# A two-layer graph network on one core: Pool's gathers wait for the slot superstep that holds the tile five (second loop: seven) tile supersteps back

## The reference, cut to what matters

```python
# layer 0
all_feat = jnp.concatenate([x[dst], x[src], edge_attr, u_per_node[dst]], axis=-1)
msg = jax.nn.relu(all_feat @ W1 + b1)
agg = jax.ops.segment_sum(msg, dst, num_segments=x.shape[0])
x = _layernorm(x + jax.nn.relu(jnp.concatenate([x, agg, u_per_node], axis=-1) @ W2 + b2))
# layer 1
Z = jnp.einsum('ni,rio->nro', h, fc_weight)
z_s = Z[src, etype]; z_d = Z[dst, etype]
e = jax.nn.relu(jnp.sum(jnp.concatenate([z_s, z_d], axis=1) * attn_weight[etype, :, 0], axis=1))
ex = jnp.exp(e - jax.ops.segment_max(e, dst)[dst])
h_out = jax.ops.segment_sum((ex / jax.ops.segment_sum(ex, dst)[dst])[:, None] * z_s, dst)
x = _layernorm(x + h_out)
```

## Time and profile before

| | us |
|---|---|
| median of 3 runs | 5624.8 |
| lowest and highest | 5622.56, 5631.35 |
| the profiled execution, its time | 5585.71 |
| its span, first to last instruction | 5584.0 |

### The profile page before, as it was taken

How to read it: one execution, slowest core, us unless ns; L and a number is a source line. 1 busy time by engine, 2 the same in 40 slices (tenths; PEclk the granted TensorE clock), 3 DMA queues, 4 the chain that set the end, 5 groups by cost and what they waited for, 6 DMA issues and landing times. The chain is left out here.

```text
span 5584.0 us, 71029 instructions
## 1 busy us (share of the span) xinstructions
PE 3080.6 (55%) x17849; PEld 2768.8 (50%) x17849; DVE 2980.1 (53%) x9486; ACT 1278.0 (23%) x4180; POOL 3034.1 (54%) x3265
## 2 busy tenths in 40 slices
PE   2265555455555555545784066555555656655576
PEld 1264444444444444444772055555555555555565
DVE  1265554455555555555773065555555555555567
ACT  0100000000000000000022044444444444444455
POOL 5525555555555555555215706666666666666631
PEclk5555555555555555555566555555555555555555
DMA  3211111111111111111125101111111111111111
GB/s 115 82 45 51 46 53 53 45 51 46 54 52 45 52 46 53 52 44 52 53 100 181 28 27 46 47 47 47 47 47 47 47 47 47 47 47 47 47 38 32
DMA packets 172540, 300.15 MB, mean 54 GB/s; under 512 B 71719, under 2 KB 78235, under 8 KB 158844
## 3 DMA queue, kind: packets, MB, share of 16 engines
q0 software_dynamic: 100032, 105.03, 9.8%
q1 hardware_dynamic: 70662, 188.25, 9.4%
q10 hardware_dynamic: 1462, 2.30, 0.1%
HBM read 260.36 MB, written 34.99 MB: 53 GB/s over the span
## 5 line engine op out<-in xcount | busy, mean ns | idle before, releaser
L453 POOL DMA_INDIRECT ring<-Btab,idx x1563 | 1486.5, 951 | 1214.7 <-DVE XA L846 610.3
L453 POOL DMA_INDIRECT ring<-Ztab,idx x1563 | 1479.9, 947 | 922.2 <-issue 400.0
L719 PE MATMUL p_m<-A,oht 128*128 x1664 | 438.3, 365 | 1061.8 <-DVE full L853 1023.5
L1344 PE MATMUL p_s<-ring,ohx 128*128 x3328 | 808.9, 420 | 191.2 <-issue 187.2
L732 PE MATMUL p_s<-msg,oh 128*128 128x64 f32 x3328 | 763.8, 418 | 178.2 <-issue 137.0
L1344 PEld LDWEIGHTS p_s<-ring,ohx 128*128 128x128 f32 x3328 | 738.8, 325 | 214.4 <-issue 214.1
L732 PEld LDWEIGHTS p_s<-msg,oh 128*128 128x128 f32 x3328 | 731.0, 329 | 204.8 <-issue 204.5
L873 DVE TENSOR_REDUCE p_t<-p_m 128x256 f32<-128x768 f32 x416 | 380.0, 958 | 817.4 <-remote 809.6
L719 PEld LDWEIGHTS p_m<-A,oht 128*128 128x128 bf16 x1664 | 237.6, 145 | 1153.8 <-issue 1109.8
L1402 DVE TENSOR_REDUCE mslot<-p_x 128x8 f32<-128x1024 f32 x208 | 254.7, 1225 | 896.8 <-remote 882.6
L632 ACT ACTIVATE msg<-p_t 128x512 f32<-128x512 f32 x208 | 124.2, 597 | 2552.7 <-issue 2161.9
(11 more groups left out here) (211 smaller groups left out, 2716.4 us busy)
## 6 DMA issues: line engine op xcount, KB each, us to landing
drow<-drow_d SPq DMA_DIRECT2D x104, 1024.0 KB
eaT<-in_eaT_in SPq DMA_DIRECT2D x208, 128.0 KB
Ztab<-Z_stage SPq DMA_DIRECT2D x49, 536.0 KB, 5.1
ring<-Btab,idx POOLq DMA_INDIRECT x1563
ring<-Ztab,idx POOLq DMA_INDIRECT x1563
xTB<-in_xTB_in SPq DMA_DIRECT2D x7, 448.0 KB, 4.0
Btab<-B_stage SPq DMA_DIRECT2D x7, 448.0 KB, 6.0
ring<-in_xTA_in SPq DMA_DIRECT2D x7, 448.0 KB, 4.2
```

What stands on the lines that cost most here:

```text
L453: e.indirect_dma_start(out=ring[:, place(t), :], out_offset=None, in_=table[:, :], in_offset=bass.IndirectOffsetOnAxis(ap=idx[:, t:t + 1], ...
L719: e.matmul(parts(j), OHT[:, s % 2, j, :], A.A3[:, bass.ds(b, 1), :].rearrange("p a c -> p (a c)"), start=True, stop=True)
L1344: last = e.matmul(pS[s % 2][h][:, j % 4, :], OHx[:, s % 2, j, :], ring[:, bass.ds(t, 1), 0:D + 1], start=True, stop=True)
```

## The change

`gathers` gets a third kind of wait, before the first tile of a tile superstep s, from s = `first` on: `used` must have reached a number from a new table, the slot superstep that holds the first slot of tile 8(s - `lead`). In the first loop `lead` is 5 and `first` 10, in the second 7 and 8. The number goes into a register, eight registers are loaded at once for eight tile supersteps, and the wait raises a semaphore `near` that nobody waits for. The old waits stay. In the first loop tile superstep 6 now also waits until `full` is 1.

The table is a new row `A.vrow` of `A.tabs`. For it the count of slots before each tile is kept in `tbef`, turned on PE with the other tables (a sixth transpose at L699 of the new file, on 13 x 128 numbers), cut to each eighth number and shifted right by 3 on DVE into 16 further columns of `rowi`, and loaded by a fourth small DMA on SP. The waits for the tables now want 80 instead of 64.

```diff
-def gathers(e, A, ring, table, idx, s_g, landed, used, summed, free={}):
-
+def gathers(e, A, ring, table, idx, s_g, landed, used, summed, near, name, lead, first, free={}):
+
+    regs = [e.alloc_register(f"{name}{j}") for j in range(O)]
...
         if s >= RT and j == 0:
             e.wait_ge(used, s - RT + BEHIND + 1)
+        if s >= first and j == 0:
+            i = (s - first) % O
+            if i == 0:
+                n = min(O, TO - s)
+                e.reg_load(regs[0:n], A.vrow[0:1, s - lead:s - lead + n])
+            e.wait_ge(used, e.snap(regs[i], min_val=1, max_val=SO)).then_inc(near, 1)
...
-            gathers(e, A, ring, A.Btab, idx, s_g, S["landed"], S["full"], S["acc"], {XT0 // O: (T["a"], len(CHUNKS))})
+            gathers(e, A, ring, A.Btab, idx, s_g, S["landed"], S["full"], S["acc"], S["near"], "l0pg", 5, 10, {6: (S["full"], 1), XT0 // O: (T["a"], len(CHUNKS))})
...
-            gathers(e, A, ring, A.Ztab, idx, s_g, S["landed"], S["s"], S["acc"])
+            gathers(e, A, ring, A.Ztab, idx, s_g, S["landed"], S["s"], S["acc"], S["near"], "l1pg", 7, 8)
...
+            e.dma_start(A.vrow.rearrange("a (c s) -> a c s", c=SC), A.rows_d[:, 3 * P + PER * WX:].unsqueeze(0)).then_inc(T["table"], 16)
...
-                last = e.transpose(pR2[:, r, :], rowsf[:, 4 + r, :], A.ident[:, :])
-            last.then_inc(T["rowt"], 1)
+                e.transpose(pR2[:, r, :], rowsf[:, 4 + r, :], A.ident[:, :])
+            e.transpose(pR2[:, 2, :], tbef[:, :], A.ident[:, :]).then_inc(T["rowt"], 1)
...
-            done(e.tensor_tensor(out=nrel[:, :], in0=w[:, :], in1=pre, op=ALU.add))
-            done(e.tensor_tensor(out=nrel[:, :], in0=nrel[:, :], in1=A.k128[:, :], op=ALU.subtract))
+            done(e.tensor_tensor(out=tbef[:, :], in0=w[:, :], in1=pre, op=ALU.add))
+            done(e.tensor_tensor(out=nrel[:, :], in0=tbef[:, :], in1=A.k128[:, :], op=ALU.subtract))
...
+            done(e.tensor_copy(rowi[:, 3 * P + PER * WX:].unsqueeze(2), by(pR2[:, 2, :])[:, :, 0:1]))
+            e.tensor_scalar(out=rowi[:, 3 * P + PER * WX:], in0=rowi[:, 3 * P + PER * WX:], scalar1=3, scalar2=None, op0=ALU.arith_shift_right)
```

More of the change, by code:

```diff
@@ L493, in phase_layer0 @@
         rowsf = sb("rows_f", [P, 6, SC], F32)
-        rowi = msg[0:SC, :, :, :].rearrange("p a j d -> p (a j d)")[:, 0:3 * P + PER * WX].bitcast(I32)
+        rowi = msg[0:SC, :, :, :].rearrange("p a j d -> p (a j d)")[:, 0:3 * P + PER * WX + PER].bitcast(I32)
         rowx = rowi[:, 3 * P:3 * P + PER * WX].rearrange("p (s w) -> p s w", w=WX)
+        tbef = sb("t_slot", [P, SC], F32)
         bf0, bl0, nt, w, nrel, n2, negm, h2, nb128 = (sb("t_" + n, [P, SC], F32) for n in (
@@ L515, in phase_layer0 @@
         pR = pM[0:SC, 0, :].rearrange("p (r k) -> p r k", r=4)
-        pR2 = pM[0:SC, 1, 0:2 * P].rearrange("p (r k) -> p r k", r=2)
+        pR2 = pM[0:SC, 1, 0:3 * P].rearrange("p (r k) -> p r k", r=3)
         pL = [pM[:, 1 + i, :].bitcast(BF16).rearrange("p (m k) -> p m k", k=P) for i in range(2)]
@@ L519, in phase_layer0 @@
         A3v = A.A3[:, 0:NB, :].rearrange("p (q h) c -> p q h c", h=2)
-        names = "oht oh c m0 m1 full pre msg s acc landed".split()
+        names = "oht oh c m0 m1 full pre msg s acc landed near".split()
         S = {n: sem("l0_" + n) for n in names}
@@ L541, in _ @@
             e.dma_start(wrow[0:1, :, :].rearrange("a (c s) w -> a c (s w)", c=SC), A.rows_d[:, 2 * P:3 * P].unsqueeze(0)).then_inc(T["table"], 16)
-            e.dma_start(xrow[0:1, :, :].rearrange("a (c s) w -> a c (s w)", c=SC), A.rows_d[:, 3 * P:].unsqueeze(0)).then_inc(T["table"], 16)
+            e.dma_start(xrow[0:1, :, :].rearrange("a (c s) w -> a c (s w)", c=SC), A.rows_d[:, 3 * P:3 * P + PER * WX].unsqueeze(0)).then_inc(T["table"], 16)
+            e.dma_start(A.vrow.rearrange("a (c s) -> a c s", c=SC), A.rows_d[:, 3 * P + PER * WX:].unsqueeze(0)).then_inc(T["table"], 16)
             e.wait_ge(T["ix"], 1)
@@ L547, in _ @@
             e.wait_ge(T["drow"], 16)
-            e.wait_ge(T["table"], 64)
+            e.wait_ge(T["table"], 80)
             rows_loaded(e, A, drow, s_dr, S["oht"], 0)
@@ L1261, in phase_layer1 @@
         pB = [pair[1][:, 512 - 3 * O:512].rearrange("p (j c) -> p j c", c=3) for pair in p_s]
-        names = "oht e ev ohe x m3 b ed ohx s0 s acc dve act ex ty landed".split()
+        names = "oht e ev ohe x m3 b ed ohx s0 s acc dve act ex ty landed near".split()
         S = {n: sem("l1_" + n) for n in names}
@@ L1618, in build @@
         A.s_typ = ctx.enter_context(nc.semaphore("typ_loaded"))
+        A.vrow = A.tabs[96:97, 0:SC * PER]
         A.s_xc = [ctx.enter_context(nc.semaphore(f"x_chunk{i}")) for i in range(len(CHUNKS))]
@@ L1692 @@
     A.drow_d = dr("drow_d", (NS, P), BF16)
-    A.rows_d = dr("rows_d", (SC, 3 * P + PER * WX), I32)
+    A.rows_d = dr("rows_d", (SC, 3 * P + PER * WX + PER), I32)
     A.ix1_d = dr("ix1_d", (P, NTP), I32)
```

## The result

The changed kernel is slower by 0.6%, little but clear of the noise: median 5660.8 us (5658.03 to 5668.22, four runs) against 5627.24 for the kernel before beside it (5622.56 to 5631.35, four runs), ratio 1.0062, 95% interval 1.0045 to 1.0079. I had forecast 5434, which is 3.4% faster.

The account below looks back on a forecast made before the run. It took Pool's long stretches of gathers, beside which TensorE's marks arrive late, to slow the kernel; 39 - 1 + 33 + 28 + 92 = 191 us off 5624.8 gave 5434, range 5385 to 5480.

Parts of the forecast that it names:

- Part 1: Before the first loop: 48 gathers without a stop instead of 80, F(0) (first addition into `full`) at 143.4; gain 39 us.
- Part 2: First loop's start: the long stretch of 104 gathers becomes 13 more ordinary supersteps; sum -1 us.
- Part 5: Second loop: gathers before the first stop fall from 184 to 64, the cycle stays; gain 92 us, 75 to 107.
- Part 4: Eleven skipped slot numbers: Pool waits one slot superstep more each time, 7 amid ongoing gathers; +28 us, between 0 and 44.
- part 3: First loop's cycle: Pool restarts 0.55 us earlier in 92 cycles, less table loads and extra waits; net +33 us.
- the lower bound: First loop's cycle: -60 us if the slow stretch catches one more of PE's results, about 1.2 us a cycle.
- My rival on the slower side: First loop: Pool stops at each superstep, after eight gathers, 16.2 us each; near 5940; chance 0.08.
- Rival 1: Only the ends gain, cycle nothing, skipped numbers 7 us each: 130 us, 5495 (5555 with lower bound); chance 0.23.
- My rival 3: Whole kernel: slow stretches are not the gathers' doing, so the change gives nothing, 5625; chance 0.05.

Follow-up runs that it names:

- the old waits begun earlier: Kernel before, its own waits from tile superstep 10 (acc: 11) instead of 23, superstep 6 waiting for the first sum: 0.9782, 5465 us; 0.9999 where before takes 4194.3.
- the doubled wait: Kernel before with its old wait at j = 0 written twice on the same number: ratio 1.0307, 5805.0 us; 1.0001 where before takes 4193.
- near wait alone: Changed kernel with its table's numbers as constants and without the old wait of j = 0: ratio 0.9696, 5462.9 us; 0.9998 where before takes 4193.
- constants with an instruction apart: Changed kernel with constants for the table's numbers, the new wait kept as an instruction of its own: ratio 0.9925; 0.9994 where before takes 4194.3.
- constants with two waits: Changed kernel with its table's numbers as constants, no register loaded, the old wait kept: ratio 0.9929, 5545 us; 1.0006 where before takes 4194.3.

## Why the prediction was wrong

**What held.** That the gathers delay the other engines in a set like this one, and that the three long runs are what is expensive: the old waits begun earlier, with nothing new in them, took off 121 us. Part 1: F(0) at 137.9, I had 143.4. Part 2: the gather of s = 10 at 202.4, I had 206. Part 5's start: the second loop's ninth superstep is gathered 104.6 us after the first gather (3075.20 - 2970.59), I had 103. Part 4: all 11 skipped numbers cost a wait; in the first loop 7 of them fall inside a run, as I had them, and these runs of 8 take 16.4 us from restart to restart (median), the 16.4 of my sum. All pauses stood where I put them. The table load of eight registers took 1.83 us in Pool's queue, three times PE's row:

```profile
L455 POOLq TENSOR_LOAD <-tabs x48: 509/1828/2032, 172.0 to 5503.0; - x48
```

The page of the Trainium skill "Runtime: NRT & Kernel Launch", section "Instruction fetch mechanics", gives about 200 ns a register, by which eight are 1.6 us, an estimate; the trace of Pool is near it, with 229 ns a register, and PE's row is not (74). So the row I took was the wrong one. It did not decide: the restarts of the changed kernel come no later behind the mark than those with constants (0.78 against 0.78 to 0.81).

**The step that failed, part 5.** "The cycle stays: Pool already stops after 8 gathers and restarts on `s` at j = 0, the new gate names the same mark of the same superstep in the cycle, and the 2.1 us of idle time there hide the table load". It names the right mark and leaves out that the wait for it now takes an instruction ahead of the gather. I looked for what would hide a *load*, and treated waits as free once their number was reached. The load is hidden, as said; the instruction is not. The 2.1 us are the time until the mark comes, and what stands between mark and gather is added behind them. 0.5 us a superstep alone would be 94 us. The even pace breaks besides, and the doubled wait shows the whole price: 3.07% of 5635, 173 us, with nothing else changed. It lies in the second loop: that is 174 us longer than before's by the profiled executions (2760.6 against 2586.5), the first 21 (2835.8 against 2815.1), and some 48 of both are the sets'. Against the near wait as the only one, the changed kernel's second loop takes 182 us more (2688.7 against 2506.3). That answers to the 194 us missing in the third row of the table, some 20 of which are the sets'. Why exactly 0.5 us turns even runs of 8 into 8, 8 and 16 I can only argue: with a later restart TensorE has more undisturbed time in each cycle, gets ahead, and its next mark comes in before the run has ended, so that Pool goes on without a stop; the run of 16 then holds up everything. The order of the idle times fits, no run takes it apart.

**The step that failed, part 3.** "the new gate would let it go at 1013.46: 0.55 us earlier in each of 92 cycles". Pool's idle time should have fallen from 6.91 to 6.36 us. It is 7.81 in the row of 985.46 above, 7.4 in the median of all stops behind runs of 16. I moved the restart and took the rest of the cycle as fixed: the addition into `full` would start 5.40 us behind the last gather's end, as in the earlier trace rows. It does not stay there. DVE's timeline in the same cycle of the changed kernel:

```profile
980.73 1.23 DVE L841 TENSOR_TENSOR oh<-p_i,dstl 128x1024 f32<-128x1024 f32 x1 [13.13 <-remote]
981.88 0.48 DVE L845 TENSOR_SCALAR oht<-drow,kcol 128x1024 bf16<-128x1024 bf16 x1
982.27 1.82 DVE L884 TENSOR_REDUCE p_t<-p_m 128x256 f32<-128x768 f32 x2
984.00 0.68 DVE L864 TENSOR_TENSOR full<-p_m,ring 128x512 f32 x1
```

The mark comes 3.1 us after the last gather's end (977.65), as in the earlier trace rows (2.9). But DVE meets it an instruction earlier in its order, at the one-hots (oh) of the superstep after instead of the reduction, so two more instructions follow before the reduction, and the addition starts 6.35 us after the run. This is what I had named as the lower bound, "if the earlier start lets the slow stretch catch one more of PE's results", and did not take. The late restart (0.78 where I gave 0.27) makes up the rest of this one row: 6.36 + 0.95 + 0.51 = 7.82.

Over the loop the two do not add up like this. The near wait alone has no second instruction and restarts 0.27 us behind the addition, and its stops are no shorter: 7.51 us in the median, with the addition 6.56 us behind the run's end; in the changed kernel these are 7.39, 0.78 and 5.9. DVE's and Pool's timeline of one such cycle, near wait alone:

```profile
360.59 1.22 DVE L837 TENSOR_TENSOR oh<-p_i,dstl 128x1024 f32<-128x1024 f32 x1 [11.10 <-remote]
...
363.86 0.68 DVE L860 TENSOR_TENSOR full<-p_m,ring 128x512 f32 x1
```

```profile
364.81 0.94 POOL L456 DMA_INDIRECT ring<-Btab,idx  x1 [7.55 <-DVE full L860]
```

And the doubled wait in the same set. Its first loop restarts on `acc` at j = 2 as before, and the second instruction, at j = 0, is in the middle of a run:

```profile
507.30 0.94 POOL L454 DMA_INDIRECT ring<-Btab,idx  x1 [7.35 <-DVE XA L847]
```

The median there is 7.34. So in one set the nearer wait made the stop 0.17 us longer and not 0.55 shorter, with no second instruction at its restarts. In the set of 5587 us the constants with an instruction apart have 7.04 in the median and the kernel before 7.05: there too nothing was gained, and the late restart cost nothing. What failed in part 3 is the gain of 51 us itself. The table of waits (engine, line waited for, us, times, longest) shows which waits moved. Changed kernel, near wait alone, doubled wait, and the old waits begun earlier:

```profile
DVE oh L841 <- remote: 944.6, 83, 13.7
```

```profile
DVE oh L837 <- remote: 1049.0, 95, 13.5
```

```profile
DVE oh L831 <- remote: 795.7, 72, 41.7
```

```profile
DVE p_t L873 <- remote: 854.0, 98, 21.4
```

The last ran in the set of 5587, the others in sets of 5627 and 5635. The third has only old waits and waits at oh as well. So the place of the wait goes with the kind of set too, not with the nearness alone; within the set of 5587 it goes with the nearness (219 us at oh with the old waits, 604 with constants).

The 78 us missing in the second row then are: 33 of part 3 that did not come; some 20 of the sets (the doubled wait's first loop takes 2835.8 us, that of before in the faster set 2815.1); some 15 for cycles 0.18 us longer than there; and some 10 for eleven stops of 1.86 us, spoken of below.

**The rivals.** My rival on the slower side (runs of eight in the first loop, 5940) did not happen. The loss was mainly in the other loop, by another mechanism, and I had no rival for it. Rival 1, "only the ends gain", was right that the cycle gives nothing and had the sign of the whole wrong. I should have asked for every wait that the diff adds on Pool which instruction carries it.

**The time itself.** With the near wait as the only one, its numbers constants, the forecast of 5434 for 5624.8, a ratio of 0.966, was met to 0.004: 0.9696. Part of that is luck: part 3's 33 us did not come there either, and some of it was made good elsewhere (before the first loop 44 us for 39; in the second loop 80 for 92, to which the slower set's share, some 25, must be added).

**Left open.** The changed kernel has ratio 1.0062 and 1.0070, constants with two waits 0.9929 and 0.9925, yet both restart 0.75 to 0.81 us after the mark. Some 75 us lie between them, against some 130 that the second instruction explains (0.9929 to 0.9696). They were measured in different sets (before at 5627 and 5630, at 5587), and the set with all of them fell on a chip where nothing shows. Whether it is the 48 loads and the register moves or the set is not settled. One thing leans to the set: behind a run of 16 in the second loop the stop is 8.5 and 7.9 us in the changed kernel's two traces, and 7.8 in the doubled wait's, which reads no register and ran where before takes 5635; with constants and two waits, where it takes 5587, it is 6.4 and 5.7. Nor is a stop of 1.86 us after a run's first gather settled (row 259.26 above), at most places each 96 gathers. It is there in the changed kernel and in those with constants and two waits; with the near wait alone the same places have 0.45 us.

## What to carry to other kernels

A wait is free only if an instruction that is there anyway can hold it. A second one in the same place, even for a number that is always reached by then, becomes an instruction between the mark and the work: 0.5 us here. Where that matters is another question: in the second loop, whose pace was even, it cost 3% of the kernel, in the first it cost nothing that shows. So when a wait is made stricter, take the weaker one out. A restart made earlier is not a cycle made shorter: look what the other engine is waiting for when it comes. And before costing a change on a profile, look whether the kernel before takes the same time in other sets: here the whole question exists on some chips only.

## What the runs showed of the hardware

**The delay beside gathers is not always there.** In three of seven sets the kernel before takes 4193 to 4195 us, and so did every other kernel in them, the changed one too. In the changed kernel there Pool gathers 1527 in a row at 1.25 us in the first loop, after 36 at its start, and all 1563 of the second; 3126 x 1.25 = 3908 us, so it is the bound. The page and two rows of the table of waits, changed kernel, such a set:

```profile
span 4190.3 us, 71831 instructions
...
PE 3198.3 (76%) x17850; PEld 2844.6 (68%) x17850; DVE 2983.1 (71%) x9488; ACT 1278.1 (31%) x4180; POOL 3030.5 (72%) x3265
```

```profile
DVE full L864 <- POOLq L443: 446.5, 158, 5.5
DVE mslot L1413 <- PE p_x L1340: 431.1, 177, 4.2
```

DVE waits for landed gathers, and in these rows for TensorE no longer than 4.2 us; no row of that table names "remote". The engines' busy times are within 2% of those of the other sets, and so is the granted clock (0.522; 0.50 and 0.52 in the two loops, the 1.2 GHz level). Only the marks come in time. My rival 3 had weighed a sentence of the Trainium skill's page "SBUF — State Buffer", section "SBUF: two separate sides", that among the engines' ports only the pair shared by VectorE and GpSimd contends and PE never waits on anyone. That is a statement on ports, and I took it for one on time: from it does not follow that TensorE's marks can't be late. No row here names a port, so no trace here speaks for the sentence or against it; what they show is late marks in four sets (944.6 us of waiting at oh, above) and none in three. What differs no profile here shows, and the chip alone is not all of it: the sets of 5587 and of 5635 us ran on the same one. The first loop's stops tell these two apart (7.05 us in the kernel before, 7.34 with the doubled wait, which restarts there on the same mark).

**Loads in Pool's queue hide behind gathers.** In that set the 48 loads of 1.83 us and a wait at each superstep cost nothing (ratio 1.0003), where I had expected 88 us and more: the gathers keep their pitch of 1.25 us. The trace shows a load lying beside them: it starts at 531.35 and takes 1.83 us, and gathers start at 530.72, 531.96 and 533.21. So the queue reads ahead of the gather that runs. Where Pool stood waiting for a mark, the wait instruction was not hidden (0.5 us at the restart).

**A second wait becomes an instruction.** The Trainium skill's page "Perfetto Trace Analysis", section "Identifying Dependency Chains", says that an instruction waiting on multiple engines may have separate semaphore instructions put before it. The 346 additional instructions of the doubled wait agree, for one semaphore waited for twice; the 0.5 us are this case's number.
